# A selective scan with mixture-of-experts tail: softplus rounds and transposed chunks interleaved, and fewer TensorE steps for router and averages

## The reference, cut to what matters

```python
# block 1, per image (B=4, L=1024 tokens, DI=192 channels, N=16 states, K=4 directions, R=24)
xh, z = split(x @ in_proj_w.T)                     # 192 + 192
xc = silu(depthwise_conv3x3(xh) + conv_b)
xs = [xc by rows, xc by columns, both flipped]     # K = 4 orders of the tokens
dts, Bs, Cs = split(x_proj_w[k] @ xs[k])           # 24, 16, 16 rows
dt = softplus(dt_projs_w[k] @ dts + dt_projs_b[k])
A  = -exp(A_logs)
h  = h * exp(dt * A) + (dt * u) * B                # over 1024 tokens, for 192 x 16 states
y  = sum_n(h * C) + D * u
y  = layernorm(sum of the four directions, put back in row order) * silu(z)
x  = x + y @ out_proj_w.T
# block 2, per token: 4 experts of 96 hidden units, top 2
probs   = softmax(xt @ router_w.T + router_b)
combine = the two largest, normalised to sum 1, else 0
out = (gelu(xt @ fc1_w[e].T + fc1_b[e]) * combine[e]) @ fc2_w[e] + combine[e] * fc2_b[e]
x   = x + out
```

## Time and profile before

| what | us |
|---|---|
| median of 3 runs (lowest 1603.81, highest 1606.59) | 1604.85 |
| the profiled execution | 1609.95 |
| its span, first to last instruction | 1608.2 |
| PE busy | 1351.8 (84%) |
| DVE busy | 1232.1 (77%) |
| ACT busy | 1011.7 (63%) |
| POOL busy | 1025.0 (64%) |

### The profile page before, as it was taken

One profiled execution on the slowest core, in us unless ns is written; L12 is line 12 of the kernel. 1 busy time (PEld: TensorE's weight loads), 2 busy tenths in 40 slices (PEclk: granted clock), 3 DMA queues, 4 the chain that ended last, 5 costly groups with the idle time before them and its releaser, 6 DMA issues. The chain is left out here.

```text
span 1608.2 us, 66443 instructions
## 1 busy us (share of the span) xinstructions
PE 1351.8 (84%) x30424; PEld 829.6 (52%) x30424; DVE 1232.1 (77%) x1025; ACT 1011.7 (63%) x1916; POOL 1025.0 (64%) x294
## 2 busy tenths in 40 slices
PE   6997679788987878888797898879787967879998
PEld 6744455454554545455464555545454533436554
DVE  4876199989798899989889998997998985742220
ACT  2458677787678778777777867777776630412222
POOL 0002089899798989989898998988899860000000
PEclk7898889999999999999999999999999987889999
DMA  9243514334233433323343342334324225101101
GB/s 322 94 155 144 169 55 112 83 84 98 68 80 88 112 76 92 99 68 91 77 112 88 80 111 70 79 75 112 94 73 127 65 79 225 40 0 40 40 35 44
DMA packets 73478, 151.08 MB, mean 94 GB/s; under 512 B 33238, under 2 KB 41942, under 8 KB 72816
## 3 DMA queue, kind: packets, MB, share of 16 engines
q1 hardware_dynamic: 73200, 146.83, 31.5%
HBM read 101.72 MB, written 32.51 MB: 83 GB/s over the span
## 5 line engine op out<-in xcount | busy, mean ns | idle before, releaser
L1213 POOL TENSOR_TENSOR s_h<-s_h,s_crow 128x2048 f32<-128x2048 f32 (+1 forms) x256 | 878.9, 3464 | 160.1 <-DVE s_h L1178 159.9
L1178 DVE TENSOR_TENSOR_SCAN s_h<-s_a,s_pb 128x1024 f32<-128x1024 f32 x384 | 864.2, 2276 | 138.4 <-PE s_pb L1006 103.1
L1006 PE MATMUL s_pb<-k_area,m_dtut 64*64 64x64 f32 x24576 | 470.9, 224 | 163.9 <-DVE s_h L1178 112.4
L1006 PEld LDWEIGHTS s_pb<-k_area,m_dtut 64*64 64x64 f32 x24576 | 426.6, 138 | 342.9 <-DVE s_h L1178 159.0
L1047 PE MATMUL s_py<-s_h,k_eye 64*64 64x512 f32 x3072 | 421.4, 604 | 16.4 <-issue 6.6
L286 ACT ACTIVATE k_area<-k_mask,m_bt 128x64 f32<-128x64 f32 x992 | 274.0, 338 | 0.0
L1104 ACT ACTIVATE s_a<-m_dup,m_aneg 128x1024 f32<-128x1024 f32 x192 | 219.4, 1143 | 28.9 <-DVE s_h L1178 28.8
L201 POOL TENSOR_TENSOR k_area<-m_bt,k_mask 128x2048 f32<-128x2048 f32 x33 | 145.7, 4418 | 129.9 <-ACT m_bt L264 129.9
L1104 ACT ACTIVATE s_a<-y_y,m_aneg 128x1024 f32<-128x1024 f32 x192 | 218.3, 1138 | 10.1 <-DVE s_h L1178 10.0
L264 ACT COPY y_y<-m_pm 128x384 f32<-128x384 f32 (+1 forms) x96 | 49.2, 513 | 104.0 <-PE m_pm L221 92.6
L1047 PEld LDWEIGHTS s_py<-s_h,k_eye 64*64 64x64 f32 x3072 | 91.9, 136 | 34.5 <-issue 23.1
(11 more groups left out here) (189 smaller groups left out, 1237.0 us busy)
## 6 DMA issues: line engine op xcount, KB each, us to landing
s_crow<-scratch_xd SPq DMA_DIRECT2D x256, 256.0 KB, 4.1
k_area<-in_x_dram SPq DMA_DIRECT2D x4, 1536.0 KB, 7.8
scratch_xt<-y_y SPq DMA_DIRECT2D x4, 1536.0 KB, 8.7
y_y<-y_y SPq DMA_DIRECT2D x24, 256.0 KB, 3.3
m_dup<-m_dup SPq DMA_DIRECT2D x24, 256.0 KB, 3.8
out_dram<-t_out SPq DMA_DIRECT2D x32, 192.0 KB, 1.9
k_area<-scratch_xt SPq DMA_DIRECT2D x3, 1536.0 KB, 6.8
scratch_xd<-h_dbl SPq DMA_DIRECT2D x8, 512.0 KB, 2.6
```

The costliest lines, as they stand in the source:

```text
L1006: mm = pe.matmul(pb[par * HALF:(par + 1) * HALF, step % 2, r * BANK + blk:(r + 1) * BANK:BLK], dtut[here, u % 2, blk, g * HALF:(g + 1) * H ...
L1178: nc.vector.tensor_tensor_scan(h[:, step % (TRIPLES * CG), f], a[:, step % RING, f], pb[:, step % 2, f], 0.0, ALU.mult, ALU.add).then_inc( ...
L1213: nc.gpsimd.tensor_tensor(here, here, c.unsqueeze(1).broadcast_to([P, groups.stop - groups.start, L]), ALU.mult).then_inc(hc_ready, 1)
```

## The change

In the scan: the UT chunks move from steps 5 to 8 to steps 7, 10, 13 and 15, and each waits for the softplus round before it, since both use `pm`. The rounds begin at steps 7, 10 and 13 instead of 9, 11 and 13. `times_u` is four instructions of two blocks each, after the scans of steps 18 to 21. In even units after the first, the sums begin two steps late, at step 9, and catch up in steps 10 and 13. The six carried pieces go to steps 11, 12, 14 and 15 of the same unit and 8 and 11 of the next. SP loads u for the D term one n later. In the tail: the router weights are padded from 4 to 32 columns; LR makes four column tiles of 256 tokens; one copy takes them to a buffer of its own; LG is two transposes of 128x128; VectorE reads the logits in four instructions; STA and STB of images 2 and 3 are one step each, with two columns per matmul.

```diff
+TURN = TT * PR // P                 # 2
+LOGITS = 64
-CAUGHT_UP = 9
-CARRIED = 6
+BEHIND = {LAG: 1, LAG + 1: 2, LAG + 2: 2, LAG + 3: 1, LAG + 4: 1, LAG + 5: 1}
+CARRIES = {(2, 11): 0, (2, 12): 1, (2, 14): 2, (2, 15): 3, (3, 8): 4, (3, 11): 5}
+ROUND_AT = (7, 10, 13)
+TIMES_AT = 18
+QUARTERS = 4
 def chunk_slot(what, i):
-    return {"Z": 0, "BT": 4, "UT": 5, "DUP": 16}[what] + i
+    return {"Z": (0, 1, 2, 3), "BT": (4,), "UT": (7, 10, 13, 15), "DUP": (16, 17, 18, 19)}[what][i]
 def chunk(self, pe, u, what, i):
         if what == "UT":
+            if u:
+                need(pe, self.dt_ready, ROUNDS * u + i)
-    def times_u(self, dve, u):
+    def times_u(self, dve, u, quarters):
+        blocks = slice(quarters.start * BLK // QUARTERS, quarters.stop * BLK // QUARTERS)
...
+        self.nc.vector.tensor_tensor(self.dtut[:, u % 2, blocks].rearrange("p k c -> p (k c)"),
+                                     self.dt_of[:, blocks].rearrange("p k c -> p (k c)"), self.ut[:, blocks].rearrange("p k c -> p (k c)"),
+                                     ALU.mult).then_inc(self.dtu_ready, len(quarters))
 # SP
-                    if n == 5 and s == 1 and o == 0:
+                    if n == 6 and s == 1 and o == 0:
                         sp.wait_ge(chunk_done, CHUNK[u + 1, "UT", 3] + 1)
                         load_u(sp, d, keep, shared, b, "skip")
 # TensorE
-            def sums(u, i):
+            def summed(u, i):
                 held = u > 0 and u % 2 == 0
+                return max(0, u * STEPS + i + 1 - LAG - (BEHIND.get(i, 0) if held else 0))
...
-                    if u % 4 == 2 and CAUGHT_UP < i <= CAUGHT_UP + CARRIED:
-                        carry(u // 4, i - CAUGHT_UP - 1)
+                    made = summed(u, i)
+                    for at in range(summed(u, i - 1), made):
+                        add_y(at // CG, at % CG)
+                    if (u % 4, i) in CARRIES:
+                        carry(u // 4, CARRIES[u % 4, i], made)
 # ScalarE
-                act.wait_ge(chunk_taken, CHUNK[u, "DUP", 0])
+                act.wait_ge(chunk_taken, CHUNK[u, "BT", 0] + 1 + (r + 1 if u % 2 == 0 else 0))
-                        if i in (9, 11, 13):
-                            logarithm(u + 1, (i - 9) // 2)
+                        if i in ROUND_AT:
+                            logarithm(u + 1, ROUND_AT.index(i))
 # VectorE
-                        if 9 <= i < 15:
-                            softplus(u + 1, (i - 9) // 2, (i - 9) % 2 * 2)
-                            softplus(u + 1, (i - 9) // 2, (i - 9) % 2 * 2 + 1)
-                        if i == 15:
-                            m.times_u(dve, u + 1)
+                        for r, at in enumerate(ROUND_AT):
+                            if at <= i < at + 2:
+                                softplus(u + 1, r, 2 * (i - at))
+                                softplus(u + 1, r, 2 * (i - at) + 1)
+                        if TIMES_AT <= i < TIMES_AT + QUARTERS:
+                            m.times_u(dve, u + 1, range(i - TIMES_AT, i - TIMES_AT + 1))
 # tail
-            between = [("STA", 2), ("STA", 3), ("STB", 2), ("STB", 3), ("LG", 1)] if b == 0 else []
+            between = {0: ("STA", 2), 2: ("STB", 2), 4: ("LG", 1)} if b == 0 else {}
+        def together(b):
+            return slice(b, BATCH) if b >= 2 else slice(b, b + 1)
 # average
-                        mm = pe.matmul(stat[:, col:col + 1], gavg[:, ci * NC + co], rhs,
+                        mm = pe.matmul(sums_of[:, b % 2:b % 2 + bs.stop - bs.start, step, co], gavg[:, ci * NC + co], rhs,
 # logit_rows
-                    for k, q in enumerate(halves()):
-                        mm = pe.matmul(buf[k * PR:k * PR + EXPERTS], wr[:, c], xn[:, b % 2, c, q], start=(c == 0), stop=(c == NC - 1))
+                    for k in range(TT // TURN):
+                        mm = pe.matmul(buf[k * PR:(k + 1) * PR, 0:TURN * P], wr[:, c], xn[:, b % 2, c, k * TURN * P:(k + 1) * TURN * P],
+                                       start=(c == 0), stop=(c == NC - 1))
 # logits: eight matmuls of 4x128 by 4x4, with a wait after four, become
+                for j in range(TURN):
+                    mm = pe.transpose(stat[:, LOGITS + j * P:LOGITS + (j + 1) * P], lrow[:, j * P:(j + 1) * P], eye[:])
 # take_rows
-                nc.scalar.copy(lrow[0:EXPERTS], buf[0:EXPERTS])
-                nc.scalar.copy(lrow[PR:PR + EXPERTS], buf[PR:PR + EXPERTS]).then_inc(small_taken, 1)
+                nc.scalar.copy(lrow[:], buf[:, 0:TURN * P]).then_inc(small_taken, 1)
 # route
-                link(V.tensor_tensor(pr[:], lg, rb[:].unsqueeze(1).broadcast_to([P, TT, EXPERTS]), ALU.add))
+                for j in range(TURN):
+                    last = V.tensor_tensor(pr[:].rearrange("p (k j) e -> p j k e", j=TURN)[:, j], lg[:, j, :, 0:EXPERTS],
+                                           rb[:].unsqueeze(1).broadcast_to([P, TT // TURN, EXPERTS]), ALU.add)
+                link(last)
```

More of the change, by code:

```diff
@@ L247, in take_chunk @@
         if what == "Z":
-            need(act, self.dtu_ready, u)
+            need(act, self.dtu_ready, QUARTERS * u)
             need(act, self.dt_ready, ROUNDS * u)
@@ L881, in _ @@
             nc.vector.scalar_tensor_tensor(zs, zs, 0.0, lnz, ALU.max, ALU.add).then_inc(m.dt_ready, ROUNDS)
-            m.times_u(dve, 0)
+            m.times_u(dve, 0, range(QUARTERS))
         @block.gpsimd
@@ L1009, in spread_b, with carry @@
                 mm.then_inc(b_row, 1)
-            def carry(b, piece):
-                first = CG * NP * 4 * b + CG * NP * 2
-                pe.wait_ge(y_added, first + CAUGHT_UP + 2 + piece - LAG)
+            def carry(b, piece, made):
+                pe.wait_ge(y_added, made)
                 if piece < 4:
@@ L1271, in tail @@
         out = sb("out", [P, 4, C])
-        lrow = keep["rows"][0:PR + EXPERTS, 0:BANK]
+        lrow = sb("lrow", [P, TURN * P])
         big = [ctx.enter_context(nc.psum_tensor(f"t_big{i}", [P, L], F32)) for i in range(2)]
@@ L1316, in stage @@
             steps += [("LR", b + 1), ("F1", b + 1, 0)] if nxt else []
-            between = [("STA", 2), ("STA", 3), ("STB", 2), ("STB", 3), ("LG", 1)] if b == 0 else []
+            between = {0: ("STA", 2), 2: ("STB", 2), 4: ("LG", 1)} if b == 0 else {}
             steps += [("LG", b + 1)] if nxt and b else []
             for t in range(TT):
-                steps += between[t:t + 1] + [("F2", b, t)]
+                steps += ([between[t]] if t in between else []) + [("F2", b, t)]
             return steps
@@ L1347, in read @@
         def read(step):
-            what, b = step
+            what, b = step[0], step[1] if step[0] == "LG" else together(step[1]).stop - 1
             return {"STA": var_stats, "STB": std_ready, "LG": lg_ready}[what], b + 1
+        def together(b):
+            return slice(b, BATCH) if b >= 2 else slice(b, b + 1)
         def op_at(b, c):
@@ L1436, in average @@
             def average(b, step):
-                pe.wait_ge((chan_stats, var_stats)[step], b + 1)
+                bs = together(b)
+                pe.wait_ge((chan_stats, var_stats)[step], bs.stop)
+                sums_of = stat[:, 0:4 * NC].rearrange("p (b s c) -> p b s c", b=2, c=NC)
                 for co in range(NC):
@@ L1441, in average @@
                     for ci in near:
-                        rhs = mv[:, b, ci, 0:1] if step == 0 else chan_var[:, b, ci:ci + 1]
-                        col = (2 * (b % 2) + step) * NC + co
-                        mm = pe.matmul(stat[:, col:col + 1], gavg[:, ci * NC + co], rhs,
+                        rhs = mv[:, bs, ci, 0] if step == 0 else chan_var[:, bs, ci]
+                        mm = pe.matmul(sums_of[:, b % 2:b % 2 + bs.stop - bs.start, step, co], gavg[:, ci * NC + co], rhs,
                                        start=(ci == near[0]), stop=(ci == near[-1]))
-                mm.then_inc((mean_sums, var_sums)[step], 1)
+                mm.then_inc((mean_sums, var_sums)[step], bs.stop - bs.start)
             def logit_rows(b):
@@ L1458, in logits @@
                 need(pe, lg_ready, b)
-                for t in range(TT):
-                    k, at = t // (TT // 2), t % (TT // 2) * P
-                    mine = slice(k * PR, k * PR + EXPERTS)
-                    mm = pe.matmul(stat[:, 64 + t * EXPERTS:64 + (t + 1) * EXPERTS], lrow[mine, at:at + P], eye[mine, mine],
-                                   start=True, stop=True)
-                    if t == TT // 2 - 1:
-                        mm.then_inc(lg_half, 1)
-                        pe.wait_ge(lg_half, b + 1)
+                for j in range(TURN):
+                    mm = pe.transpose(stat[:, LOGITS + j * P:LOGITS + (j + 1) * P], lrow[:, j * P:(j + 1) * P], eye[:])
                 mm.then_inc(lg_done, 1)
```

27 lines of the change are left out of this document (7 added, 20 removed).

## The result

The changed kernel takes 1642.5 us (median of six runs), the kernel before 1606.7 beside it: a ratio of 1.021 (1.017 to 1.025). It is slower by some 34 us; the forecast was 1594 us and the range ended at 1604. The profiled execution took 1639.4 us, with a span of 1637.7. The scan takes 1162.7 us in it (before: 1123.6), so +39.1; what lies behind takes 287.1 in place of 295.1.

The account below looks back on a forecast made before the run. No engine was taken as full in the scan, so waits between engines bound it; behind it TensorE did. Scan +1.2 and tail -12.0 gave -10.8 us, off the median 1604.85: 1594, range 1570 to 1604 for 8 in 10.

Parts of the forecast that it names:

- Three more instruction starts at 0.09 ... are +0.26.: Scan, dt*u in four on VectorE: splitting costs only three extra instruction starts, +0.26 us a unit.
- The chunk at step 15, +0.75 an odd unit: Odd units, TensorE: chunk of u behind the third round 0.15, dt chunks at 16 and 17 0.6; range 0 to 1.7.
- The new wait for the logarithm, 33 us: First round at step 7: VectorE waits for ScalarE's logarithm, 2.6 us in odd units, 0.45 to 3.65 in even ones.
- Rival B: Scan, step 7: no stall at round 0, 1561 us, with half of it 1577; chance 0.15, the half included.
- Cover, -7.5 (0 to -15): Scan, steps 18 to 21: dt*u in four gives TensorE time and hides half of 15 us of VectorE's waits.
- the -3.5 forecast: Odd units: moving chunks of u from steps 5 to 8 to between the rounds removes four times 0.87 us.
- the sign that was named for C and D: Scan, last eight steps: VectorE waiting longer for TensorE there would show the forecast wrong.
- rival C: Scan: dt*u in four hides no waits and step 15's chunk costs its upper end; 14 us more, 1608; chance 0.15.
- the +1.2 forecast: Whole scan: all costs and gains there, less 7.5 us of cover, sum to +1.2 us, ends -32 and +24.
- Rival D, slower: Scan, steps 15 to 19 meet GpSimd's mask build; its backlog makes TensorE wait; 15 us more, 1623; chance 0.08.
- Rival E: Tail: the logits' transposes leave TensorE at its lower clock level; 3.6 us more, 1598; chance 0.07.
- The tail, -12.0 (-6 to -15): Behind the scan: logit rows -3.9, logits -5.2, averages -2.9 us.

Follow-up runs that it names:

- Experiments 1 and 3: Kernel before with only dt*u in quarters: ratio 1.015; changed kernel with quarters not multiplying by u: 1630.5 us as a product with a constant, 1610.1 as a reduction.
- Experiment 5: Changed kernel with dt*u in halves at steps 19 and 21 and chunks of u at 5, 7, 10, 13, none behind the last round: 1597.9 us, ratio 0.993.
- experiment 6: dt*u whole at step 15, chunks of u at 5, 7, 10, 13: 1605.7 us; then ScalarE's mask rows also taken out of steps 4 to 7: 1583.7.
- one_later: Kernel with dt*u in halves and no chunk of u behind the last round, its rounds moved one step later, to 8, 11, 14: 1598.1 us, ratio 0.993.
- reduce_quarters: Changed kernel whose four dt*u quarters are a reduction over one element with one SBUF input, not a product with u: 1610.1 us in one run.

## Why the prediction was wrong

**The step that failed: "Three more instruction starts at 0.09 ... are +0.26."** It priced a quarter as a quarter of 1.73 us, a duration that the trace shows at step 15 alone. There, in all 15 units, dt*u starts just as GpSimd's instruction ends. The time line of GpSimd in the kernel before, unit 9, shows the hint:

```profile
867.75 6.88 POOL L1213 TENSOR_TENSOR s_h<-s_h,s_crow 128x2048 f32<-128x2048 f32 x2 [3.66 <-DVE s_h L1178]
874.59 5.17 POOL L201 TENSOR_TENSOR k_area<-m_bt,k_mask 128x2048 f32<-128x2048 f32 x1
```

GpSimd ends at 874.63, dt*u runs from 874.54 to 876.27, and the mask build beside it takes 5.17 us, where the median of the changed kernel's is 3.63: it waited 1.5. Moved to steps 18 to 21, the same product meets GpSimd's long instructions: +3.56 us a unit (81.1 less 27.7, over 15) for +0.26. Experiments 1 and 3 show cause and price.

**The chunk at step 15, +0.75 an odd unit.** Steps 15 to 17 take 9.74 us on average in odd units and 6.55 in units 4, 8 and 12, which have no chunk there: 3.2, beyond the upper end of 1.7. The queue behind the chunk was right: in unit 13, where the clock stayed at 1.00, it is 1.3 us, inside the range. The lower clock behind TensorE's idle was not in the sum: in units 5, 7 and 9, at 0.62, it is 4.2. Experiment 5 takes both away.

**The new wait for the logarithm, 33 us: right,** in its sum and in most units: 34.2 us in 20 waits, 29.3 more than the 4.9 of before; at step 7 most odd units wait 2.83 us (2.6 forecast), units 4 and 8 wait 3.65 (3.65), and units 2, 6, 10 and 14 wait 0.42 (0.45). In experiment 6 it cost about its length, some 20 us for 20; in experiment 5 the 5.8 us of one_later brought nothing. Rival B falls.

**Cover, -7.5 (0 to -15): right for quarters that do not wait.** In reduce_quarters, where each takes 0.53 us as the prediction had it, the waits for products in scans 18 to 23 fall from 20.7 to 12.2 us, by 8.5. Quarters that wait for GpSimd give TensorE more time: in the changed kernel the same waits fall by 17.1, and those in scans 0 to 5 by 14.5, which the prediction did not count. Before scans 6 to 9 of odd units, where the chunks of u lay, 20.5 us go (-2.9 a unit for the -3.5 forecast). The chunk at step 15 brings 19.0 back in scans 15 to 17; the rest is small, and in all it is the 34.5 us. So in the last eight steps VectorE waits 22.5 us for 20.7, the sign that was named for C and D, but nearly all of it is the chunk's. Of rival C the cover did not fail, and the chunk went beyond the price that C gave it.

**The sum.** In the scan VectorE's busy time grows from 1011.8 to 1056.3 us, +44.5 (dt*u's 53.4, less, for the most part, overlaps with the instructions beside it); its waits change by +29.3 and -34.5, in all its idle by -5.4: +39.1, for the +1.2 forecast.

**Rival D, slower,** had the sign and not the mechanism. VectorE and GpSimd do meet, but one instruction at a time, and GpSimd has no growing backlog: its waits for VectorE's scans rise from 159.9 to 213.2 us. Only at the scan's end is it late, by 3.7 us. **Rival E** falls: over 3.0 us behind the transposes the clock is 1.00.

**The tail, -12.0 (-6 to -15).** Its own stretch gives -16.3, beyond the range: logit rows 3 x 1.50 for 2.74, 4.44 and 2.74, -5.4 (the 4.44 lay at a granted clock of 0.62; at full clock 2.74 becomes 1.50, 1.24 less for the 1.3 taken); logits -5.3; averages -3.2; and the rest, 2.4, fits the granted clock of the stretch, 0.98 for 0.96. The lower clock behind the logits was seen in the earlier trace rows and left out of the sum. The change got -8.0, since the stretch ahead lost 8.3; that this falls inside the range is luck, two misses of opposite sign. VectorE reads the logits of an image in two instructions, not in four, which changes nothing in the sum.

## What to carry to other kernels

Ahead of moving a VectorE instruction with two SBUF inputs, look at what GpSimd does at the new place: its duration at the old place is a price only for that meeting. An instruction that is longer than its like, on either engine, may hold a wait which no list of waits shows. When work is spread to give TensorE time, what stands behind it in TensorE's order must be there already, or its idle and a lower clock may take the time back, as they did here in six of seven units.

## What the runs showed of the hardware

VectorE's product with a constant, SBUF to SBUF with one input, waited for GpSimd like the product of two tensors (1.29 and 1.32 us on average for 384 columns), though alone it took 0.47 to 0.49, little less than the reduction's 0.53. That is shown for columns read in the order `p c k` alone. The clock behind TensorE's idle of 2.8 us at step 15 was not the same each time: over 9 us it was 0.62 in units 5, 7 and 9, 0.81 in units 1, 3 and 11, and 1.00 in unit 13; what decides between them stays open.
